# Two-layer attention and expert block on one core: score masks at the end of a group of banks, diagonals cleared on GpSimd, and a new order of expert pieces

## The chip, the cores and the metric

The program runs on one core of one Trainium2 chip. The metric is the device time of one launch in microseconds, lower is better.

## What is computed

The input is x with 8 batches of 512 tokens of 256 features. Two layers follow each other, and each adds an attention and a mixture of experts, both computed from the same normalized input:

```python
xn = _layernorm(x)
x = x + L0_attn(xn) + L0_ffn(xn)   # 16 heads of 16; softmax; 8 experts, each token takes 4
xn = _layernorm(x)
x = x + L1_attn(xn) + L1_ffn(xn)   # sparsemax attention; L1_ffn: grouped-query attention, then 8 experts, each token takes 2
# each attention: causal scores of 512 x 512 for every head
scores = q @ k.T * scale            # masked above the diagonal
attn = softmax(scores)              # L1_attn: maximum(scores - tau, 0), tau from the sorted row (sparsemax)
ctx = attn @ v
# each expert: out = down(act(gate(x)) * up(x))
```

So there are three attentions over 8 batches and 16 heads (the first layer's, called "mla" in the kernel, the grouped-query one, "gqa", and the sparsemax one, "spm") and two layers of experts.

## The kernel before

**Pairs.** The kernel walks through 192 pairs of heads G: 8 pairs for each batch n = G // 8, first the 8 batches of mla, then of gqa, then of spm. p = G % 8 is the pair's place in its batch. The order of all instructions is written out by hand: each engine has its own program (TensorE as `pe`, VectorE as `dve`, ScalarE as `act`, GpSimd as `pool`, the loads on `sp`), they go through the pairs in the same order, and semaphores join them.

**Scores.** A pair has its scores twice. The "q" scores (line 586) have queries in the partitions; VectorE takes their row maxima (`maxima`, lines 1800 and 1798, the latter a MAX8 for sparsemax). The "k" scores (line 589) have keys in the partitions; ScalarE turns them into the probabilities `pt` (`probabilities`, line 1447), and TensorE multiplies `pt` by V (`outputs`, line 658). Each kind is 6 units, 3 for each of the two heads j, of 512, 512 and 256 columns, and each unit fills one PSUM bank. In front of the scores of a unit stands a mask matmul (line 579), which puts the large negative values above the diagonal into the bank (`start=True`); the scores then add to it. VectorE's maxima of pair G + 1 and ScalarE's probabilities of pair G are made in the same round.

**Banks.** PSUM has 8 banks. A `Ring` hands out the banks of S (scores) and of X (transposes, projections, outputs) in turn; whoever takes a bank waits until its former user has read it (`S.former`). In a pair without experts ("alone") both rings have 4 banks; in a pair with experts X has 2 and S has 3 (banks 5 to 7), and banks 2 to 4 take the expert matmuls:

```python
wide, narrow = (banks[0:4], banks[4:8]), (banks[0:2], banks[5:8])
```

**Experts.** The tokens are sorted into tiles of 256, 71 tiles in the first layer and 39 in the second. A tile is six pieces: gate, up and down, each for m = 0 and 1; each piece is 12 matmuls of 256 columns (line 533 for gate and up, line 553 for down). `plan` lays them into pairs: 15 pieces in each of the pairs 21 to 49 (mla) and 6 in each of the pairs 138 to 176 (spm). The pieces of a pair are cut into the six parts q = 0 to 5 of `pair_with_experts`, between which the pair's scores, transposes and outputs stand. After the up piece VectorE makes the product t (line 1648), ScalarE its high part ah (line 1350), and GpSimd the low part al (`low`, line 1128); the down piece of the same tile and m reads both. `xl` (line 1603) is the low part of a tile's input.

**The rest of the round.** `turn_qk` transposes q and k of pair G + 1 (line 507) once GpSimd has stacked them (`stack`, lines 1161 to 1180). `outputs_by_rows` turns the outputs back (line 507, oT). `project` makes the next batch's projections. In the first pairs GpSimd also makes square roots by powers (`head_rms`, lines 1204 and 1210), which VectorE's `norm_heads` (line 1749) waits for, and scatters token rows for the experts (`route_scatter`, line 1264, 8 scatters in each of the pairs 3 to 18).

Of the kernel before, what the change touches and what calls it, by code (L numbers as in the profile page):

```python
# [23 lines left out]
P = 128  # L24
# [4 lines left out]
ALU = mybir.AluOpType  # L29
# [4 lines left out]
B, T, D = 8, 512, 256  # L34
# [24 lines left out]
FIRST_GATHERS = 55  # L59
KINDS = ["mla"] * B + ["gqa"] * B + ["spm"] * B  # L60
# [16 lines left out]
PT_AT = {0: 0, 3: 512, 1: 640, 2: 1024}  # L77
# [70 lines left out]
def build(nc, dram, outs, ctx):  # L148
# [232 lines left out]
    def pipeline(kinds, its, mems, em=None, general=False):  # L381
# [49 lines left out]
        dve_step, pool_step = new("dve_step"), new("pool_step")  # L431
# [46 lines left out]
        scatter_at = {2 * b + 3 + half: [(b, half)] for b in range(B) for half in range(2)} if em else {}  # L478
# [7 lines left out]
        with block as block:  # L486

            @block.tensor
            def _(pe):
# [68 lines left out]
                def experts(G, q):  # L558
                    for what, s, i in plan[G][q]:
# [7 lines left out]
                def scores(which, G, units):  # L567

                    mem = mems[kinds[G // NP]]
                    for u in units:  # L570
                        name = (which, G, u)
                        S.add(name, "dve" if which == "q" else "act")
                        if S.former[name]:
                            pe.wait_ge(*S.former[name])
                        bank = S.bank(name)
                        unit = (Q_UNITS if which == "q" else K_UNITS)[u]

                        diag = min(first + (P * blk if which == "q" else 0) for _, blk, first, _ in unit)
                        pe.matmul(bank[:, diag:diag + P * len(unit)], ident_bf[:, :],  # L579
                                  masks_bf[:, 0 if which == "q" else 1, 0:len(unit), :].rearrange("p n k -> p (n k)"),  # L580
                                  start=True, stop=False, skip_group_check=True)
                        for n, (j, blk, first, width) in enumerate(unit):
                            end = n == len(unit) - 1
                            ks = mem["ksT"][key_at[G] % 2][j]
                            if which == "q":
                                mm = pe.matmul(bank[:, first:first + width], mem["qsT"][:, P * blk:P * (blk + 1)],  # L586
                                               ks[:, 0:width], start=False, stop=end, skip_group_check=True)
                            else:
                                mm = pe.matmul(bank[:, first:first + width], ks[:, P * blk:P * (blk + 1)],  # L589
                                               mem["qaT"][:, T - width:T], start=False, stop=end, skip_group_check=True)  # L590
                        mm.then_inc(s_full, 1)
# [54 lines left out]
                def outputs(G):  # L646
# [3 lines left out]
                    pe.wait_ge(s_act, S.count[("k", G, NU - 1)])  # L650
# [114 lines left out]
                def pair_with_experts(G):  # L765
# [28 lines left out]
                    experts(G, 5)  # L794
                    if is_at(n - 1, "spm") and p == 1:
                        attention_out(n - 1)
                    if nxt and 1 <= p <= NT:
                        project(n + 1, p - 1)
# [70 lines left out]
            def _(sp):  # L869
# [56 lines left out]
                def experts(G, q):  # L926
                    for what, s, i in plan[G][q]:
# [193 lines left out]
            def _(pool):  # L1121
# [9 lines left out]
                def experts(G, q):  # L1131
# [1298 lines left out]
```

## Time and profile before

| | before |
|---|---|
| time, median of 3 runs | 3224.46 us (3221.11 to 3225.25) |
| the profiled execution | 3229.72 us, span 3227.9 us, mean granted TensorE clock 0.956 |
| busy: PE, PEld | 2843.6 us (88%), 2276.0 us (71%) |
| busy: DVE, ACT, POOL | 2161.9 us (67%), 1622.1 us (50%), 1399.3 us (43%) |
| mask matmuls, line 579 | 2304, 581.2 us busy (matmuls overlap in the records) |

PE is TensorE's matmul, PEld its weight load, DVE is VectorE, ACT is ScalarE and POOL is GpSimd. Matmuls are pipelined, and their modelled durations overlap: the distance from one start to the next says what one costs. The pairs begin and end as follows (read from the first score matmul of each): pairs 0 to 20 alone, 0 to 423.9 us; pairs 21 to 49 with experts, to 1385.8; pairs 50 to 137 alone, to 2313.8; pairs 138 to 176 with experts, to 3055.4; pairs 177 to 191 alone, to 3227.9.

### The profile page before, as it was taken

What the parts mean: (1) busy time and instruction counts of PE and PEld (TensorE: products, weight loads), DVE (VectorE), ACT (ScalarE), POOL (GpSimd) and SP (SyncE); (2) the same over time, 40 slices, a digit from 0 to 9 for tenths busy, and PEclk for the clock granted to TensorE, in tenths of its full rate; (3) what the DMA queues carried; (4) which work ended last, traced back from release to release, by engine and by line L of the source; (5) the groups of instructions that cost most, each with busy time, mean ns of one, the idle gap of its engine ahead of it and who ended that gap; (6) DMA issues with size and microseconds to landing.
All of it is one profiled execution on the core that took longest, in us unless ns stands there. A gap on an engine that the chain in (4) does not pass through costs nothing. (4 is left out here: it accounts for less than half of the span.)

```text
span 3227.9 us, 61041 instructions
## 1 busy us (share of the span) xinstructions
PE 2843.6 (88%) x21398; PEld 2276.0 (71%) x21398; DVE 2161.9 (67%) x6229; ACT 1622.1 (50%) x3388; POOL 1399.3 (43%) x1941
## 2 busy tenths in 40 slices
PE   3877789999999999979888888898799999999986
PEld 1555578888888888856666666666588888888864
DVE  3876778678777767756777777766645544454576
ACT  1544444444444454445555555565455545545553
POOL 3587742343233233275556666322222222222377
PEclk8878899999999999989999999999899999999999
DMA  2465567678777777613333334210365555565445
GB/s 80 143 232 185 203 242 304 260 267 316 278 271 278 273 289 271 255 30 61 94 92 106 106 105 106 90 67 22 138 226 197 221 200 203 197 228 193 137 99 125
DMA packets 192067, 580.11 MB, mean 180 GB/s; under 512 B 22857, under 2 KB 144657, under 8 KB 157457
## 3 DMA queue, kind: packets, MB, share of 16 engines
q1 hardware_dynamic: 154896, 525.03, 44.1%
q0 software_dynamic: 36864, 51.14, 7.7%
q8 instruction: 175, 2.87, 0.3%
q14 instruction: 132, 1.07, 0.1%
HBM read 450.14 MB, written 125.96 MB: 178 GB/s over the span
## 5 line engine op out<-in xcount | busy, mean ns | idle before, releaser
L1128 POOL TENSOR_TENSOR al<-t,ah 128x512 fp32r<-128x512 f32 x220 | 285.6, 1298 | 989.4 <-ACT ah L1350 989.4
L579 PE MATMUL bank<-masks_bf,ident_bf 128*128 128x128 bf16 (+1 forms) x2304 | 581.2, 252 | 113.9 <-DVE st L1800 52.8
L533 PE MATMUL bank<-xh,gu 128*128 128x256 f32 x3520 | 628.3, 285 | 10.0 <-issue 5.1
L1800 DVE TENSOR_REDUCE st<-bank 128x1 f32<-128x512 f32 (+3 forms) x1024 | 422.2, 480 | 202.3 <-PE bank L586 202.1
L1447 ACT ACTIVATE pt<-bank 128x512 f32<-128x512 f32 (+1 forms) x1152 | 511.4, 540 | 91.2 <-PE bank L589 89.7
L533 PEld LDWEIGHTS bank<-xh,gu 128*128 128x128 f32 x3520 | 505.2, 190 | 19.6 <-issue 13.5
L579 PEld LDWEIGHTS bank<-masks_bf,ident_bf 128*128 128x128 bf16 x2304 | 225.6, 98 | 391.6 <-DVE st L1800 112.6
L586 PE MATMUL bank<-ksT,qsT 128*128 128x512 f32 (+3 forms) x1536 | 438.1, 382 | 0.0
L589 PE MATMUL bank<-qaT,ksT 128*128 128x512 f32 (+3 forms) x1536 | 435.3, 392 | 0.0
L1455 ACT ACTIVATE oT<-bank 128x512 f32<-128x512 f32 x192 | 114.4, 596 | 547.9 <-PE bank L658 547.9
L533 PE MATMUL bank<-xl,gu 128*128 128x256 f32 x1760 | 352.5, 282 | 0.0
L507 PE MATMUL bank<-ident,qst 128*128 128x128 f32 x1536 | 239.5, 284 | 82.6 <-POOL kst L1180 52.7
L1350 ACT ACTIVATE ah<-t 128x512 fp32r<-128x512 f32 x220 | 138.8, 631 | 309.4 <-DVE t L1641 271.9
L586 PEld LDWEIGHTS bank<-ksT,qsT 128*128 128x128 f32 x1536 | 285.3, 206 | 4.0 <-issue 1.3
L589 PEld LDWEIGHTS bank<-qaT,ksT 128*128 128x128 f32 x1536 | 281.3, 204 | 0.0
L553 PE MATMUL bank<-dn,ah 128*128 128x256 f32 x1760 | 259.8, 291 | 22.3 <-issue 13.6
L533 PEld LDWEIGHTS bank<-xl,gu 128*128 128x128 f32 x1760 | 272.0, 190 | 0.0
L507 PEld LDWEIGHTS bank<-ident,qst 128*128 128x128 f32 x1536 | 183.9, 146 | 120.7 <-POOL kst L1180 62.4
L658 PE MATMUL bank<-pt,V 128*17 128x512 f32 (+3 forms) x3072 | 260.8, 460 | 0.7 <-ACT pt L1447 0.7
L1798 DVE MAX8 top<-bank 128x8 f32<-128x512 f32 (+3 forms) x512 | 213.2, 482 | 55.2 <-PE bank L586 52.4
L553 PEld LDWEIGHTS bank<-dn,ah 128*128 128x128 f32 x1760 | 227.3, 192 | 31.6 <-issue 31.6
L1224 POOL DMA_INDIRECT acc<-ys_scratch,slots x128 | 203.3, 1588 | 44.0 <-issue 43.6
(253 smaller groups left out, 5124.7 us busy)
## 6 DMA issues: line engine op xcount, KB each, us to landing
gu<-wu_scratch SPq DMA_DIRECT2D x110, 2056.0 KB, 7.9
dn<-wd_scratch SPq DMA_DIRECT2D x110, 1024.0 KB, 9.5
xs<-xs_scratch SPq DMA_DIRECT2D x110, 264.0 KB, 9.0
ys_scratch<-yb SPq DMA_DIRECT2D x110, 256.0 KB, 9.8
raw<-in_gu SPq DMA_DIRECT2D x16, 1024.0 KB, 5.6
wu_scratch<-hi SPq DMA_DIRECT2D x16, 1024.0 KB, 9.5
wu_scratch<-lo SPq DMA_DIRECT2D x16, 1024.0 KB, 12.8
xs_scratch<-empty SPq DMA_DIRECT2D x32, 264.0 KB, 5.3
```

The source lines that it names most:

```text
L507: mm = pe.transpose(bank[:, P * n:P * (n + 1)], b, ident[:, :])
L533: mm = pe.matmul(bank[:, TS * h:TS * (h + 1)], gu[:, col:col + P], x[s % 2][:, TS * k:TS * (k + 1)], start=(n == 0), stop=(n == len(terms) ...
L553: mm = pe.matmul(down_bank[:, D * half:D * (half + 1)], a[s % 2][:, j // 2, tok:tok + P], dn[:, part + D * j:part + D * (j + 1)], start=(n ...
L579: pe.matmul(bank[:, diag:diag + P * len(unit)], ident_bf[:, :], masks_bf[:, 0 if which == "q" else 1, 0:len(unit), :].rearrange("p n k -> ...
L586: mm = pe.matmul(bank[:, first:first + width], mem["qsT"][:, P * blk:P * (blk + 1)], ks[:, 0:width], start=False, stop=end, skip_group_che ...
L589: mm = pe.matmul(bank[:, first:first + width], ks[:, P * blk:P * (blk + 1)], mem["qaT"][:, T - width:T], start=False, stop=end, skip_group ...
L658: mm = pe.matmul(bank[q0:q0 + HD + 1, P * kb:T], V[n % 2][:, kb, vh, :], pt[:, j, PT_AT[kb]:PT_AT[kb] + T - P * kb], start=(kb < 2), stop= ...
L1128: pool.tensor_tensor(em["al"][s % 2][:, m, :], em["t"][g % 2][:, :], em["ah"][s % 2][:, m, :].bitcast(F32), ALU.subtract).then_inc(al_read ...
L1224: pool.indirect_dma_start(acc[:, NT * b + t, :], None, ys_dram, at, compute_op=ALU.add).then_inc(gathered[i], 16)
L1447: act.activation(to, frm, ACT.Relu if kind == "spm" else ACT.Exp).then_inc(s_act, 1)
L1798: ins = dve.max(top[:, 0, r, :], bank[:, first:first + width])
L1800: ins = dve.reduce_max(st[:, 0, r:r + 1], bank[:, first:first + width], AX.X)
```

## The change

Six parts of code change.

1. `scores` takes its units in groups, of 3 units where S has 3 banks and of 2 where it has 4. All waits for the group's banks stand before its first matmul. Then come the scores of all its units, and at the end one mask matmul for each unit, which now adds to the scores; only this last one tells the reader that the bank is full.
2. In pairs with experts (68 pairs) the k units are `bare`: they have no mask matmul. GpSimd's new `clear` sets the entries of `pt` above the diagonal to zero with four affine_selects of 256 columns per pair, and `outputs` waits for these (`pt_ready`). The blocks of `pt` lie in another order (`PT_AT`) so that two diagonal blocks can be reached with one stride. The clears stand on GpSimd behind the low parts of part q = 2.
3. In the first layer the pieces of a tile go gate 0, up 0, gate 1, down 0, up 1, down 1, where before they went gate, up, down, gate, up, down (the downs are those of the tile before).
4. In mla pairs with experts, `project` (and ScalarE's `take_projected`) stands before the last piece of part q = 5, not behind it.
5. The scatters of pairs 3 to 18 are 10, 5, 5, 10, 10, 8, 10, 5, 5, 5, 5, 10, 12, 12, 12 and 4, where before they were 8 in each; the sum is 128 as before.
6. `norm_heads(0, 4:H)` on VectorE stands behind the maxima and the shift of pair 1, where before it stood ahead of pair 0.

The core of the diff (the other engines' `experts` take the same slice):

```diff
@@ constants
+FIRST_SCATTERS = (10, 5, 5, 10, 10, 8, 10, 5, 5, 5, 5, 10, 12, 12, 12, 4)
-PT_AT = {0: 0, 3: 512, 1: 640, 2: 1024}
+PT_AT = {0: 0, 2: 512, 3: 768, 1: 896}
@@ plan
-                for m in range(2):
-                    work += [("gate", s, m), ("up", s, m)] if cur else []
-                    work += [("down", s - 1, m)] if prev else []
+                ups = [[("gate", s, m), ("up", s, m)] if cur else [] for m in range(2)]
+                downs = [[("down", s - 1, m)] if prev else [] for m in range(2)]
+                if layer == 0:
+                    work += ups[0] + ups[1][:1] + downs[0] + ups[1][1:] + downs[1]
+                else:
+                    work += ups[0] + downs[0] + ups[1] + downs[1]
@@ PE, scores
-                    for u in units:
-                        name = (which, G, u)
-                        S.add(name, "dve" if which == "q" else "act")
-                        if S.former[name]:
-                            pe.wait_ge(*S.former[name])
-                        bank = S.bank(name)
...
+                    bare = which == "k" and G in plan
+                    side, width_of = 0 if which == "q" else 1, Q_UNITS if which == "q" else K_UNITS
+                    size = 3 if len(S.banks) == 3 else 2
+                    for group in [units[i:i + size] for i in range(0, len(units), size)]:
+                        for u in group:
+                            S.add((which, G, u), "dve" if which == "q" else "act")
+                            if S.former[(which, G, u)]:
+                                pe.wait_ge(*S.former[(which, G, u)])
+                        for u in group:
+                            bank, unit = S.bank((which, G, u)), width_of[u]
+                            for n, (j, blk, first, width) in enumerate(unit):
...
+                            if bare:
+                                mm.then_inc(s_full, 1)
+                        for u in group if not bare else ():
+                            bank, unit = S.bank((which, G, u)), width_of[u]
+                            diag = min(first + (P * blk if which == "q" else 0) for _, blk, first, _ in unit)
+                            pe.matmul(bank[:, diag:diag + P * len(unit)], ident_bf[:, :],
+                                      masks_bf[:, side, 0:len(unit), :].rearrange("p n k -> p (n k)"),
+                                      start=False, stop=True, skip_group_check=True).then_inc(s_full, 1)
@@ PE, outputs
-                    pe.wait_ge(s_act, S.count[("k", G, NU - 1)])
+                    if G in plan:
+                        pe.wait_ge(pt_ready, 4 * (1 + sorted(plan).index(G)))
+                    else:
+                        pe.wait_ge(s_act, S.count[("k", G, NU - 1)])
@@ PE, pair_with_experts (ACT's has the same with take_projected)
-                    experts(G, 5)
...
+                    if is_at(n, "mla"):
+                        experts(G, 5, slice(0, -1))
+                        if nxt and 1 <= p <= NT:
+                            project(n + 1, p - 1)
+                        experts(G, 5, slice(-1, None))
+                    else:
+                        experts(G, 5)
...
@@ POOL
+                def clear(G, j):
+
+                    pt = mems[kinds[G // NP]]["pt"]
+                    pool.wait_ge(s_act, S.count[("k", G, NU // 2 * (j + 1) - 1)])
+                    for first, size in ((0, 1024), (768, 256)):
+                        blocks = pt[:, j, first:first + size].rearrange("p (n q) -> p n q", n=2)[:, :, 0:P]
+                        pool.affine_select(out=blocks, in_=blocks, pattern=[[0, 2], [1, P]], compare_op=ALU.is_ge, fill=0.0,
+                                           base=0, channel_multiplier=-1).then_inc(pt_ready, 1)
...
                     if G in plan:
-                        for q in range(2, 6):
+                        experts(G, 2)
+                        clear(G, 0)
+                        clear(G, 1)
+                        for q in range(3, 6):
                             experts(G, q)
...
-                    for b, half in scatter_at.get(G, ()):
-                        route_scatter(b, half)
+                    for b, t, k in scatter_at.get(G, ()):
+                        route_scatter(b, t, k)
@@ DVE
+                    if G == 0 and is_at(0, "mla"):
+                        norm_heads(0, slice(4, H))
...
-                if kinds[0] == "mla":
-                    norm_heads(0, slice(4, H))
                 for G in range(steps):
```

The first place is TensorE in a pair alone, at the q scores of the next pair (ksT and qsT are the keys and the queries, the numbers in names only tell buffers and semaphores apart, and s_dve and s_act count the banks that VectorE and ScalarE have read). Before:

```order
L579 MATMUL bank<-masks_bf,ident_bf 128x128 [waits s_act_301,k_half_309,cast_170]
L586 MATMUL bank<-ksT_53,qsT 128x512
L579 MATMUL bank<-masks_bf,ident_bf 128x256 [waits s_act_301]
L586 MATMUL bank<-ksT_53,qsT 128x384
L586 MATMUL bank<-ksT_53,qsT 128x128
L579 MATMUL bank<-masks_bf,ident_bf 128x128 [waits s_act_301]
L586 MATMUL bank<-ksT_53,qsT 128x256
L579 MATMUL bank<-masks_bf,ident_bf 128x128 [waits s_act_301]
L586 MATMUL bank<-ksT_54,qsT 128x512
L579 MATMUL bank<-masks_bf,ident_bf 128x256 [waits s_dve_302]
```

After the change:

```order
L590 MATMUL bank<-ksT_53,qsT 128x512 [waits s_act_301,k_half_310,cast_170]
L590 MATMUL bank<-ksT_53,qsT 128x384
L590 MATMUL bank<-ksT_53,qsT 128x128
L601 MATMUL bank<-masks_bf,ident_bf 128x128
L601 MATMUL bank<-masks_bf,ident_bf 128x256
L590 MATMUL bank<-ksT_53,qsT 128x256 [waits s_act_301]
L590 MATMUL bank<-ksT_54,qsT 128x512
L601 MATMUL bank<-masks_bf,ident_bf 128x128 x2
L590 MATMUL bank<-ksT_54,qsT 128x384 [waits s_dve_302]
L590 MATMUL bank<-ksT_54,qsT 128x128
L590 MATMUL bank<-ksT_54,qsT 128x256
```

The two masks of a group moved behind the last score matmul of the group, and where a group's second bank is waited for, the wait stands ahead of the first bank's matmuls too.

The second place is TensorE in a sparse pair with experts, at the q scores of the next pair on both sides of a down piece (line 553 before is line 559 after; dn is the down weight, ah and al the two parts of the activation). Before:

```order
L579 MATMUL bank<-masks_bf,ident_bf 128x128 [waits s_act_301,k_half_309,cast_170]
L586 MATMUL bank<-ksT_55,qsT 128x512
L579 MATMUL bank<-masks_bf,ident_bf 128x256 [waits s_act_301]
L586 MATMUL bank<-ksT_55,qsT 128x384
L586 MATMUL bank<-ksT_55,qsT 128x128
L579 MATMUL bank<-masks_bf,ident_bf 128x128 [waits s_act_301]
L586 MATMUL bank<-ksT_55,qsT 128x256
L553 MATMUL bank<-dn_108,ah_88 128x256 [waits y_used_370,al_ready_368]
L553 MATMUL bank<-dn_108,ah_88 128x256 x7
L553 MATMUL bank<-dn_108,al_90 128x256 x4
L579 MATMUL bank<-masks_bf,ident_bf 128x128 [waits s_dve_302]
```

After the change:

```order
L590 MATMUL bank<-ksT_55,qsT 128x512 [waits s_act_301,k_half_310,cast_170]
L590 MATMUL bank<-ksT_55,qsT 128x384
L590 MATMUL bank<-ksT_55,qsT 128x128
L590 MATMUL bank<-ksT_55,qsT 128x256
L601 MATMUL bank<-masks_bf,ident_bf 128x128
L601 MATMUL bank<-masks_bf,ident_bf 128x256
L601 MATMUL bank<-masks_bf,ident_bf 128x128
L559 MATMUL bank<-dn_108,ah_88 128x256 [waits y_used_371,al_ready_369]
L559 MATMUL bank<-dn_108,ah_88 128x256 x7
L559 MATMUL bank<-dn_108,al_90 128x256 x4
L590 MATMUL bank<-ksT_56,qsT 128x512 [waits s_dve_302]
```

The masks stand as a block behind the scores of the three units, and the second half begins with a score matmul, ahead of which the waits of all three banks stand, where before it began with the mask of its first bank.

The third place is GpSimd in a sparse pair with experts (kst is the stack of keys, pt the probabilities). Before:

```order
L1177 MEMSET qst_50 128x8x2
L1180 COPY kst<-kst 128x8x16 [waits pool_step_304]
L1128 TENSOR_TENSOR al_90<-t_95,ah_88 128x512 [waits ah_ready_367]
L1128 TENSOR_TENSOR al_91<-t_94,ah_89 128x512 [waits ah_ready_367]
L1161 CAST qst_49<-qk_69 128x8x16 [waits loaded_169]
```

After the change:

```order
L1201 COPY kst<-kst 128x8x16 [waits pool_step_304]
L1149 TENSOR_TENSOR al_90<-t_95,ah_88 128x512 [waits ah_ready_368]
L1209 AFFINE_SELECT pt<-pt 128x2x128 [waits s_act_301]
L1209 AFFINE_SELECT pt<-pt 128x256
L1209 AFFINE_SELECT pt<-pt 128x2x128 [waits s_act_301]
L1209 AFFINE_SELECT pt<-pt 128x256
L1149 TENSOR_TENSOR al_91<-t_94,ah_89 128x512 [waits ah_ready_368]
```

Four clears were added between the low part of one piece and that of the next; the first of each two waits for ScalarE's probabilities of one head.

## Rows read from the trace of the kernel before

**Rows 1.** Windows, the five stages: us, busy of PE, PEld, DVE, ACT, POOL, PEclk, DMA share, GB/s.

```profile
0.00:423.90 423.90, 291.32 (x1700) 202.72 (x1704) 285.61 (x841) 178.33 (x363) 281.60 (x324) 0.81 0.49 173
423.90:1385.80 961.90, 891.06 (x7245) 807.97 (x7238) 712.84 (x1641) 447.55 (x882) 320.85 (x366) 0.99 0.72 272
1385.80:2313.80 928.00, 813.16 (x5872) 568.26 (x5876) 680.95 (x2175) 527.20 (x1188) 482.96 (x741) 0.96 0.30 82
2313.80:3055.40 741.60, 714.57 (x5615) 604.80 (x5608) 367.92 (x1208) 384.30 (x781) 183.47 (x359) 0.99 0.55 203
3055.40:3227.90 172.50, 133.47 (x977) 92.20 (x975) 114.58 (x366) 84.72 (x179) 130.38 (x154) 0.96 0.53 108
```

**Rows 2.** Timeline of PE in a pair alone: start, us, engine, line, what.

```profile
1502.29 0.22 PE L579 MATMUL bank<-masks_bf,ident_bf 128*128 128x128 bf16 x1
...
1504.31 0.23 PE L579 MATMUL bank<-masks_bf,ident_bf 128*128 128x128 bf16 x1
...
1504.64 1.27 PE L658 MATMUL bank<-pt,V 128*17 128x512 f32 x16
1505.85 0.23 PE L579 MATMUL bank<-masks_bf,ident_bf 128*128 128x128 bf16 x1
...
1507.88 0.38 PE L507 MATMUL bank<-ident,oT 128*128 128x128 f32 x2
```

**Rows 3.** Timeline of DVE and ACT in the same pair.

```profile
1502.90 3.27 DVE L1800 TENSOR_REDUCE st<-bank 128x1 f32<-128x512 f32 x8 [1.85 <-PE bank L586]
...
1506.47 2.62 ACT L1447 ACTIVATE pt<-bank 128x512 f32<-128x512 f32 x6
```

**Rows 4.** Waits of PEld, pairs 50 to 137: total us, times, longest.

```profile
PEld bank L579 <- DVE st L1800: 74.6, 192, 3.7
...
PEld bank L579 <- ACT ksT L1434: 25.5, 31, 1.2
```

**Rows 5.** Timeline of PE in a sparse pair with experts.

```profile
2535.98 0.23 PE L579 MATMUL bank<-masks_bf,ident_bf 128*128 128x128 bf16 x1
...
2537.00 0.40 PE L533 MATMUL bank<-xh,gu 128*128 128x256 f32 x2
2537.24 0.40 PE L533 MATMUL bank<-xl,gu 128*128 128x256 f32 x2
...
2538.43 0.23 PE L579 MATMUL bank<-masks_bf,ident_bf 128*128 128x128 bf16 x1
...
2539.39 1.11 PE L553 MATMUL bank<-dn,ah 128*128 128x256 f32 x8
...
2540.82 0.23 PE L579 MATMUL bank<-masks_bf,ident_bf 128*128 128x128 bf16 x1
...
2543.27 1.27 PE L658 MATMUL bank<-pt,V 128*17 128x512 f32 x16
...
2548.10 0.63 PE L507 MATMUL bank<-ident,oT 128*128 128x128 f32 x4 [1.06 <-DVE xl L1603]
```

**Rows 6.** Timeline of DVE and POOL in the same pair.

```profile
2539.58 3.48 DVE L1798 MAX8 top<-bank 128x8 f32<-128x512 f32 x8
...
2540.11 1.28 POOL L1128 TENSOR_TENSOR al<-t,ah 128x512 fp32r<-128x512 f32 x1 [3.21 <-ACT ah L1350]
```

**Rows 7.** Groups of GpSimd's instructions: busy us, mean ns, idle before.

```profile
L1180 POOL COPY kst<-kst 128x128 f32<-128x128 f32 x160 | 48.6, 304 | 10.1
```

**Rows 8.** Waits of PE, pairs 21 to 49.

```profile
PE bank L507 <- DVE xl L1603: 15.8, 8, 2.1
PE bank L553 <- issue: 13.6, 15, 1.2
...
PE bank L553 <- POOL al L1128: 4.7, 6, 0.8
...
PE bank L533 <- DMA gu<-wu_scratch: 2.1, 3, 1.2
```

**Rows 9.** Waits of all engines, pairs 0 to 20.

```profile
DVE qk_mla L1749 <- POOL qkn L1210: 15.6, 2, 13.0
```

More of the change, by code:

```diff
@@ L477, in pipeline @@
         per_batch = 16 * NT * CHOICES[0]
-        scatter_at = {2 * b + 3 + half: [(b, half)] for b in range(B) for half in range(2)} if em else {}
+        scatters = [(b, t, k) for b in range(B) for t in range(NT) for k in range(CHOICES[0])]
+        scatter_at = {3 + i: scatters[sum(FIRST_SCATTERS[:i]):sum(FIRST_SCATTERS[:i + 1])]
+                      for i in range(len(FIRST_SCATTERS))} if em else {}
         def routes(G, lag):
@@ L556, in down, with experts @@
                     mm.then_inc(y_full, 1)
-                def experts(G, q):
-                    for what, s, i in plan[G][q]:
+                def experts(G, q, some=slice(None)):
+                    for what, s, i in plan[G][q][some]:
                         if what == "gate":
@@ new lines, in scores @@
+                    bare = which == "k" and G in plan
[9 more added lines that the diff above has]
+                            for n, (j, blk, first, width) in enumerate(unit):
+                                end = bare and n == len(unit) - 1
+                                ks = mem["ksT"][key_at[G] % 2][j]
+                                if which == "q":
+                                    mm = pe.matmul(bank[:, first:first + width], mem["qsT"][:, P * blk:P * (blk + 1)],
+                                                   ks[:, 0:width], start=(n == 0), stop=end, skip_group_check=True)
+                                else:
+                                    mm = pe.matmul(bank[:, first:first + width], ks[:, P * blk:P * (blk + 1)],
+                                                   mem["qaT"][:, T - width:T], start=(n == 0), stop=end,
+                                                   skip_group_check=True)
+                            if bare:
[6 more added lines that the diff above has]
+                                      start=False, stop=True, skip_group_check=True).then_inc(s_full, 1)
@@ L924, in store_y, with experts @@
                     sp.dma_start(ys_blocks[s - FIRST_TILE[layer_of(s)]], em["yb"][s % 2][:, :, :]).then_inc(y_out[s % 2], 16)
-                def experts(G, q):
-                    for what, s, i in plan[G][q]:
+                def experts(G, q, some=slice(None)):
+                    for what, s, i in plan[G][q][some]:
                         if what == "up" and s + 2 < tiles_to(s):
@@ L1129, in low, with experts @@
                                        em["ah"][s % 2][:, m, :].bitcast(F32), ALU.subtract).then_inc(al_ready, 1)
-                def experts(G, q):
-                    for what, s, i in plan[G][q]:
+                def experts(G, q, some=slice(None)):
+                    for what, s, i in plan[G][q][some]:
                         if what == "up":
@@ L1364, in take_y, with experts @@
                                    scale=em["wsel"][s % 3][:, half:half + 1]).then_inc(y_used, 1)
-                def experts(G, q):
-                    for what, s, i in plan[G][q]:
+                def experts(G, q, some=slice(None)):
+                    for what, s, i in plan[G][q][some]:
                         if what == "up":
@@ L1506, in pair_with_experts @@
                     take_o(G)
-                    experts(G, 5)
-                    if n + 1 < nb and 1 <= p <= NT:
-                        take_projected(n + 1, p - 1)
+                    if is_at(n, "mla"):
+                        experts(G, 5, slice(0, -1))
+                        if n + 1 < nb and 1 <= p <= NT:
+                            take_projected(n + 1, p - 1)
+                        experts(G, 5, slice(-1, None))
+                    else:
+                        experts(G, 5)
+                        if n + 1 < nb and 1 <= p <= NT:
+                            take_projected(n + 1, p - 1)
                     if G + 1 in ends_at:
@@ L1649, in multiply, with experts @@
                                           ALU.mult).then_inc(a_ready, 1)
-                def experts(G, q):
-                    for what, s, i in plan[G][q]:
+                def experts(G, q, some=slice(None)):
+                    for what, s, i in plan[G][q][some]:
                         if what == "gate":
```

42 lines of the change are left out of this document (13 added, 29 removed).

## The prediction

> **What bounds the kernel now.** I read the windows first, cut at the pairs where the kernel changes its manner [rows 1]. TensorE is busy in 93 to 96% of the two stretches with experts (891 of 962 us, 715 of 742), in 88% of pairs 50 to 137 alone, and in 69% of the first. So where experts run the time is what TensorE has to issue, and a matmul taken out is time won unless a wait takes its place. Alone, TensorE and VectorE (681 of 928 us) hand PSUM banks to each other, and it is the handing over that counts.
>
> The timeline of one pair alone shows that [rows 2, 3]. The q scores begin at 1502.29 and end where the outputs begin, 1504.64: 2.35 us for 6 units. VectorE's first maximum begins at 1502.90, 0.61 later, and its 8 reductions then run on end for 3.27 us, 0.41 each. The last unit (1504.31) waits for a bank whose maxima end at 1502.90 plus the first three reductions and some signalling, 1.41 after VectorE's start. The k scores last from 1505.85 to 1507.88, 2.03 us; ScalarE starts 0.62 after them and reads 2560 columns in 2.62 us. The chain of the round goes q scores, outputs, k scores, transposes, all on TensorE. The waits of the weight loads say that this pair is typical: 192 waits at line 579 for VectorE's maxima, over two per pair [rows 4]. Of the 88 pairs, 31 wait for ksT as well, 25.5 us in all: there a delay of TensorE's scores can be partly absorbed.
>
> In a sparse pair with experts, call T the start of the first q half, 2538.43 [rows 5, 6]. A half of q scores costs 0.96 (to the down piece at 2539.39), a k half 1.02 (2535.98 to 2537.00), and a matmul of 256 columns 0.12 (two from 2537.00 to 2537.24). VectorE's maxima begin at T+1.15 and run on end for 3.48 us through both halves; the second q half begins on TensorE at T+2.39, the outputs at T+4.84. GpSimd's low part ends at T+2.96.
>
> **The change, pair by pair.**
>
> *Groups in pairs alone (part 1).* The same matmuls are issued, but a bank is full only when the whole group of two has been scored. At 0.12 us per 256 columns the first group's 1024 columns take 0.24 + 0.18 + 0.12 = 0.54 before the first mask, where before the first bank's last matmul was issued at 0.03 and took a slot to 0.35. The first bank is therefore full some 0.25 later, and VectorE starts at about 0.86 rather than 0.61. It needs the same 1.41 until the second bank is free, and the third group, which now waits for both banks ahead of its first matmul, starts at 2.27. Its 384 + 128 + 256 columns and two masks take about 0.66, so the q scores end at 2.93: **+0.58**. Likewise for k: ScalarE starts at 0.87 and has read the first two units (1024 of 2560 columns) 1.05 later; with the signal the third group starts at 2.0 and ends at 2.66: **+0.63**. I take 1.15 a pair, 101 us over 88 pairs. What absorbs it is the pairs that wait for ksT or for GpSimd: about half of the 25.5 us and a little more, 15. **Pairs 50 to 137: +86.** The last 15 pairs, partly bound by GpSimd's gathers (130 of 172 us busy [rows 1]), get 0.85 each: **+13**. The bounds are 0 (if everything else in the round were late enough) and the full 1.2, which is 124 over 103 pairs.
>
> By the Trainium skill (TensorE: Matmul & The Clock Gate, back-to-back issue gap) a stream of weight loads and matmuls of 128 columns goes at 81 ns each, where the rows here show 0.11 to 0.12; by it the third groups would be some 0.1 shorter each, and the sum about 18 us less. The row decides.
>
> *Masks out of the k halves with experts (part 2).* Bare, a k half is 1280 columns, 0.60 to 0.66, against 1.02: 0.38 won, 0.76 a pair. In pairs 21 to 49, 29 pairs, **−22**. VectorE's q maxima there have two or three pieces of 1.4 us between the halves, so a group of three waits for nothing.
>
> *Order of pieces and projection (parts 3, 4).* Down pieces in pairs 21 to 49 wait 13.6 (put down to issue, but ahead of a matmul that waits for al) and 4.7 us for GpSimd [rows 8]. With another piece between up and down this goes, −18. But a_ready, by which the next gate weights are loaded, comes one piece later for one of two pieces; three waits for gu already exist, 2.1 us, so the slack is thin. I give half back, +9: **−9**. The waits for xl (15.8) stay: the projection's move only changes which instruction meets them. Stage sum **−31**; bounds −15 (all of the waits come back) and −42.
>
> *Sparse pairs with experts (parts 1, 2).* The masks again give 0.76. Against it, the second q half now waits for all three banks at once, that is for the maxima of the whole first half: T+1.15+1.74 = T+2.89, where TensorE arrives at T+2.36. So it stalls 0.53, and VectorE then idles until the second half's first mask, but ends its maxima at about T+5.5, ahead of what needs them. Net some −0.16 a pair. The down piece's product t and the transposes (the wait of 1.06 at 2548.10) follow TensorE and shift with it. 39 pairs: **−6**.
>
> *The clears.* No row shows an affine_select. Each is 256 columns; the nearest rows are a copy of 128 columns, 0.304 [rows 7], and a two-input operation of 512, 1.28 [rows 6]: bounds 0.30 and 1.3; a line through both gives 0.63 for 256, which I take. Four of them behind the low part end at T+2.96+2.52 = T+5.48; TensorE reaches the outputs at T+4.84+0.53 = T+5.38. So 0.1 of wait, with the signal 0.16: **+6** over 39. They fall free below 0.6; from there each 0.1 us costs 0.4 a pair, 16 us. In pairs 21 to 49 two and a half times the pieces lie in between, and GpSimd is busy 321 of 962 us: hidden. The next low part stands behind the clears, but its down piece is a pair later.
>
> By the Trainium skill (GPSIMD Engine Reference, 3.1 Elementwise) an element costs about 2.6 cycles with two inputs, 1.8 in the best loop; at 1.2 GHz that is 0.38 to 0.55 us for 256 columns, and the clears would be hidden. For the 512-column row with two inputs it gives 1.11 us, and the row has 1.28; no row here shows a one-input select, so the line stands.
>
> *First pairs (parts 5, 6).* VectorE stands 13.0 us in norm_heads behind GpSimd's powers with the maxima of pair 1 ready behind it [rows 9]. Moved, it does some 5 us of that work in the gap: **−5**. The scatters have the same sum, and GpSimd is busy 282 of 424 us there [rows 1]; I count neither their spreading nor the group's lateness, since those pairs wait for GpSimd. Bounds −12 and +8.
>
> Sum: +86 + 13 − 31 − 6 + 6 − 5 = **+63** on the profiled execution of 3229.7 us, 5.3 above the median of the runs: 3224.5 + 63 = 3287; I say **3286**.
>
> **The rivals.**
>
> *A, the forecast: TensorE waits in the third groups.* For it: the banks' turn is fixed, and 192 waits stand there already. Own range: 0.9 to 1.2 a pair alone and the bounds of the other terms, 3255 to 3320. Chance 0.66.
>
> *B, the clears are dear.* At 1.0 us each they end at T+6.96, and the outputs wait 1.58 a pair, 62 us over 39 in place of 6: 3342. For it: the two-input row, 1.28 for 512 columns, if most of it were a fixed cost [rows 6]; against it: the copy's 0.304, which bounds what is fixed [rows 7]. It decides from 0.9 up. Chance 0.12.
>
> *C, the groups cost half.* If the round alone is held by something else, the 0.45 left are 46 us over 103 pairs, against −36 from the rest: 3234. Against it: 88% of TensorE busy. Chance 0.12.
>
> *D, faster.* The place is the same third group: if the delay of VectorE's start is only 0.1 (a mask at the end is short, and VectorE could be let in sooner after it than after a score matmul of 512) and the third group's start is met by banks free earlier, a pair alone loses 0.2, 21 us, against −36, with cheap clears −6 more: 3203 to 3210. It decides from 0.35 us a pair alone down (36 / 103). Against it: the wait for the second bank exists today, and nothing makes it shorter. Chance 0.10.
>
> **How the numbers follow.** The likeliest is A, 3286. The range must leave out no more than 2 in 10: it drops D and the outer half of B and takes in C: 3232 to 3338. This kernel's measurement tells 0.2%, 6.4 us, from no change. Slower is A, B and most of C, 0.86; C's lower end gives 0.05 within 0.2%; D is 0.09 and over.
>
> **What the profile of the changed kernel would show.** Alone: q scores of 2.9 us and k scores of 2.65, with waits of the third group for st and for pt; stretches of about 1014 us for pairs 50 to 137 and 186 for the last. Pairs 21 to 49 in 931 us, with new waits for gu and few at the down piece. Pairs 138 to 176 in 742, with VectorE idle about 0.9 us between its two groups of MAX8, and a short wait of the outputs for GpSimd; the affine_select at 0.63 us. First stretch 419. The prediction is wrong if the pairs alone are not longer by 0.9 or more, or if an affine_select takes over 0.9 us.

## The result and the profile after

The changed kernel takes 3316.62 us (median of 4 runs, 3313.60 to 3321.54), the kernel before 3222.78 us, measured beside it: the ratio is 1.0288, with an interval of 1.0271 to 1.0305. It is slower by 94 us; the forecast was 3286 us, in a range of 3232 to 3338.

The page of the changed kernel begins so (share of the span, count of instructions):

```profile
span 3314.7 us, 61380 instructions
...
PE 2793.5 (84%) x20990; PEld 2293.6 (69%) x20990; DVE 2177.6 (66%) x6229; ACT 1647.5 (50%) x3388; POOL 1499.9 (45%) x2213
```

TensorE has 408 matmuls less, and the span is 86.8 us longer: the work went down and the waiting up. The windows, cut at the same pairs as [rows 1] (the cuts ahead of pairs 21 and 138 lie 0.1 to 0.3 us behind the start of the outputs of the pair before, and not at a first score matmul; they do so in every run below, so the stretches compare):

```profile
0.00:425.20 425.20, 288.87 (x1700) 204.01 (x1704) 288.12 (x841) 182.34 (x363) 281.13 (x324) 0.84 0.51 178
425.20:1353.30 928.10, 864.99 (x7070) 807.31 (x7062) 717.21 (x1641) 447.47 (x881) 366.50 (x482) 0.99 0.75 279
1353.30:2377.10 1023.80, 806.60 (x5872) 581.68 (x5876) 690.22 (x2175) 545.48 (x1187) 484.41 (x741) 0.96 0.28 75
2377.10:3125.00 747.90, 695.32 (x5378) 603.07 (x5379) 366.57 (x1208) 383.56 (x781) 239.13 (x514) 1.00 0.54 200
3125.00:3314.70 189.70, 137.70 (x981) 97.51 (x979) 115.53 (x366) 88.62 (x179) 128.72 (x154) 0.94 0.48 98
```

| pairs | before | forecast | after | difference, forecast and measured |
|---|---|---|---|---|
| 0 to 20, alone | 423.9 | 419 | 425.2 | −5, +1.3 |
| 21 to 49, experts | 961.9 | 931 | 928.1 | −31, −33.8 |
| 50 to 137, alone | 928.0 | 1014 | 1023.8 | +86, +95.8 |
| 138 to 176, experts | 741.6 | 742 | 747.9 | 0, +6.3 |
| 177 to 191, alone | 172.5 | 186 | 189.7 | +13, +17.2 |

Every stretch of pairs alone is longer. In pairs 50 to 137 the instructions are as many as before and the granted clock is the same (0.96 both times); in the first pairs it was 0.84 against 0.81, in the last 0.94 against 0.96. The pair alone of [rows 2, 3], in the timeline of the changed kernel:

```profile
1479.42 0.85 PE L590 MATMUL bank<-ksT,qsT 128*128 128x512 f32 x3
1480.11 0.34 PE L601 MATMUL bank<-masks_bf,ident_bf 128*128 128x128 bf16 x2
...
1480.44 3.38 DVE L1837 TENSOR_REDUCE st<-bank 128x1 f32<-128x512 f32 x8 [2.05 <-PE bank L601]
...
1481.94 0.64 PE L590 MATMUL bank<-ksT,qsT 128*128 128x384 f32 x3 [1.01 <-DVE st L1837]
1482.42 0.34 PE L601 MATMUL bank<-masks_bf,ident_bf 128*128 128x256 bf16 x2
1482.69 1.27 PE L673 MATMUL bank<-pt,V 128*17 128x512 f32 x16
1483.89 0.79 PE L593 MATMUL bank<-qaT,ksT 128*128 128x512 f32 x3
...
1484.85 1.85 ACT L1478 ACTIVATE pt<-bank 128x512 f32<-128x512 f32 x4 [0.22 <-PE bank L601]
...
1486.08 0.64 PE L593 MATMUL bank<-qaT,ksT 128*128 128x128 f32 x3 [0.74 <-ACT pt L1478]
1486.56 0.34 PE L601 MATMUL bank<-masks_bf,ident_bf 128*128 128x256 bf16 x2
1486.73 0.61 PE L513 MATMUL bank<-ident,oT 128*128 128x128 f32 x4
```

The q scores take 3.27 us (1479.42 to 1482.69) where they took 2.35, the k scores 2.84 where they took 2.03. In each, the third group stands and waits: 1.01 us for VectorE, 0.74 for ScalarE. VectorE starts 1.02 us after the first score matmul, where it started 0.61 after the first mask. The waits of TensorE over pairs 50 to 137 (us in all, times, longest) say that it is so throughout:

```profile
PE bank L590 <- DVE st L1837: 91.0, 77, 3.7
PE bank L593 <- ACT pt L1478: 61.5, 88, 1.0
PE bank L590 <- DVE top L1835: 19.7, 11, 5.3
```

The first and the third line are the waits for VectorE's maxima (st, and top in sparse pairs), 77 and 11, one in each of the 88 pairs; in the kernel before TensorE's matmuls waited 26.7 us in 13 waits for st and 6.7 in 3 for top. The second line, again one wait in each pair, has no counterpart among the matmuls of the kernel before. Its weight loads did wait for ScalarE's pt, 83 times and 13.0 us in all; they now do 88 times, 74.6 us.

The pair shown is one of the first layer's attention. In the 64 grouped-query pairs alone (64 to 127), which are most of the 88, the medians counted from the traces are 0.89 us from the first score matmul to VectorE's start (0.61 before), 3.14 for the q scores (2.36) and 2.84 for the k scores (2.03).

A sparse pair with experts, to be read beside [rows 5, 6]:

```profile
2604.10 0.86 PE L590 MATMUL bank<-ksT,qsT 128*128 128x512 f32 x4
...
2605.52 1.68 DVE L1835 MAX8 top<-bank 128x8 f32<-128x512 f32 x4
...
2606.06 1.27 POOL L1149 TENSOR_TENSOR al<-t,ah 128x512 fp32r<-128x512 f32 x1 [3.12 <-ACT ah L1381]
...
2607.28 1.49 POOL L1209 TENSOR_SCALAR_AFFINE_SELECT pt<-pt 128x256 f32<-128x256 f32 x4
...
2607.35 0.87 PE L590 MATMUL bank<-ksT,qsT 128*128 128x512 f32 x4 [0.67 <-DVE top L1835]
...
2608.33 1.69 DVE L1835 MAX8 top<-bank 128x8 f32<-128x512 f32 x4 [1.13 <-PE bank L601]
2609.81 1.27 PE L673 MATMUL bank<-pt,V 128*17 128x512 f32 x16
```

VectorE's maxima, one run of 3.48 us before, are two runs with 1.13 us of idle time between them, and the second q half waits 0.67 for the first. The four clears take 1.49 us together and are done at 2608.77, 1.04 before the outputs at 2609.81. Over the whole of pairs 138 to 176 no wait of the outputs for GpSimd is in the trace, so the clears hold TensorE up nowhere there.

### The profile page after: what moved, and what is told of

It reads as the page before. It is cut to its first block and busy times, and to the rows that moved or that the text cites. A ratio compares the mean times of both kernels' runs of the same rounds, so it can differ in the third digit from the quotient of the medians.

```text
span 3314.7 us, 61380 instructions
## 1 busy us (share of the span) xinstructions
PE 2793.5 (84%) x20990; PEld 2293.6 (69%) x20990; DVE 2177.6 (66%) x6229; ACT 1647.5 (50%) x3388; POOL 1499.9 (45%) x2213
## 5 line engine op out<-in xcount | busy, mean ns | idle before, releaser
L539 PE MATMUL bank<-xh,gu 128*128 128x256 f32 x3520 | 654.9, 290 | 19.4 <-DMA gu<-wu_scratch 5.7
L1478 ACT ACTIVATE pt<-bank 128x512 f32<-128x512 f32 (+1 forms) x1152 | 522.4, 529 | 90.6 <-PE bank L601 65.0
L1837 DVE TENSOR_REDUCE st<-bank 128x1 f32<-128x512 f32 (+3 forms) x1024 | 430.1, 481 | 205.9 <-PE bank L601 203.4
L590 PE MATMUL bank<-ksT,qsT 128*128 128x512 f32 (+3 forms) x1536 | 366.2, 353 | 223.9 <-DVE st L1837 124.4
L590 PEld LDWEIGHTS bank<-ksT,qsT 128*128 128x128 f32 x1536 | 259.0, 197 | 286.4 <-DVE st L1837 139.0
L593 PE MATMUL bank<-qaT,ksT 128*128 128x512 f32 (+3 forms) x1536 | 362.0, 350 | 91.4 <-ACT pt L1478 90.6
L593 PEld LDWEIGHTS bank<-qaT,ksT 128*128 128x128 f32 x1536 | 237.4, 194 | 153.4 <-ACT pt L1478 108.9
L601 PE MATMUL bank<-masks_bf,ident_bf 128*128 128x128 bf16 x1896 | 301.6, 248 | 0.0
L673 PE MATMUL bank<-pt,V 128*17 128x512 f32 (+3 forms) x3072 | 270.2, 474 | 0.5 <-ACT pt L1478 0.5
L1182 POOL CAST qst<-qk 128x128 fp32r<-128x128 f32 x128 | 45.0, 351 | 390.4 <-PE bank L513 381.1
```

Of the source, the lines that this page charges most:

```text
L539: mm = pe.matmul(bank[:, TS * h:TS * (h + 1)], gu[:, col:col + P], x[s % 2][:, TS * k:TS * (k + 1)], start=(n == 0), stop=(n == len(terms) ...
L673: mm = pe.matmul(bank[q0:q0 + HD + 1, P * kb:T], V[n % 2][:, kb, vh, :], pt[:, j, PT_AT[kb]:PT_AT[kb] + T - P * kb], start=(kb < 2), stop= ...
L1478: act.activation(to, frm, ACT.Relu if kind == "spm" else ACT.Exp).then_inc(s_act, 1)
L1837: ins = dve.reduce_max(st[:, 0, r:r + 1], bank[:, first:first + width], AX.X)
```

## The experiments

Each run changes one thing in the kernel that it starts from; the comparisons by stretch are between single profiled executions. e1 to e4 ran on one chip, e5 to e8 on a second, e9 and e10 on a third; the kernel before took 3242.28, 3226.22 and 3226.27 us on them, and no execution of it was profiled on the first. Stretches with the same code came out up to 6 us apart in pairs 50 to 137 (922.4 in e7, 922.5 in e5, 924.2 in e6, 926.0 in e8, 927.9 in e10 and 928.0 in the kernel before, which all have the same scores there), 7 us apart in pairs 21 to 49 (928.1 in the changed kernel, 935.4 in e2), 4 us apart in pairs 0 to 20 and 1 us apart in pairs 138 to 176. Only more than that is read as a difference.

**One unit in a group, everywhere (e1) and in pairs alone only (e2).**

```diff
-                    size = 3 if len(S.banks) == 3 else 2
+                    size = 1                                   # e1
+                    size = 3 if len(S.banks) == 3 else 1       # e2
```

> The changed kernel with groups of one unit everywhere: each unit waits for its own bank, then come its scores and its mask. All else stays. My theory (banks are told full too late and waited for too early) gives pairs 50 to 137 about 930 us (1023.8 in the changed kernel), the last 15 pairs 173 to 177 (189.8), pairs 138 to 176 about 730 (747.8), since the stall of the second q half goes too, pairs 21 to 49 unchanged at 928: a span of about 3190. The rival, that the loss in pairs alone lies in what is left of the change there (the mask adding to the scores rather than the scores to the mask, the other layout of pt), leaves pairs 50 to 137 above 1000 and the span above 3290.

> Groups of one unit in pairs alone only; pairs with experts keep groups of three. My theory: pairs 50 to 137 at 930 us, the last pairs at 175, pairs 138 to 176 still 748, a span of about 3207. The difference of pairs 138 to 176 to the run with one unit everywhere is what the group of three costs there: I expect 15 to 20 us. If the rival is right that the clears or the layout of pt take back what the masks gave in pairs 138 to 176, both runs have the same 748 there.

e1 took 3190.7 us, a ratio of 0.9844 (0.9827 to 0.9860) to the kernel before. Its pairs 50 to 137 take 939.1 us, its last pairs 171.0 and pairs 138 to 176 718.6. e2 took 3230.11 us, with 935.9, 174.8 and 748.1. So the groups are the loss in pairs alone: 85 of the 96 us. With experts the groups of three cost 748.1 − 718.6 = 29.5 us, where I had expected 15 to 20. The whole of e2 is longer than I expected too, a span of 3228.3 us against 3207, because its pairs 0 to 20 (434.1) and 21 to 49 (935.4) are. The rival that the clears or the layout of pt hold the sparse pairs falls with e1's 718.6. What is open is that the pairs 50 to 137 of e1 and e2 are still 11 and 8 us above the kernel before.

**The two halves of a group: early waits only (e3), late masks only (e4).** In e3 each unit's mask follows its scores; in e4 each unit's wait stands ahead of its own scores.

```diff
 # e3: the mask moves into the loop over scores
-                        for u in group if not bare else ():
...
+                            if not bare:
...
+                                pe.matmul(bank[:, diag:diag + P * len(unit)], ident_bf[:, :],
 # e4: one loop for waits and scores
                             if S.former[(which, G, u)]:
                                 pe.wait_ge(*S.former[(which, G, u)])
-                        for u in group:
                             bank, unit = S.bank((which, G, u)), width_of[u]
```

> Groups as in the changed kernel, but only their waits stand together: each unit's mask follows its scores at once, so a bank is told full as soon as before. In pairs alone VectorE should start some 0.3 us sooner than in the changed kernel, and the third group still waits for two banks. By my step-by-step sum a pair alone then loses 0.9 rather than 1.6 us against the kernel before: pairs 50 to 137 at about 985 us. If the early waits cost nothing by themselves, they come to 930; if they are the whole loss, to 1020.

> Groups as in the changed kernel, but each unit waits for its own bank ahead of its own scores; the masks stay at the group's end. In pairs alone the first unit of the third group can be scored while the second bank is still read, but its mask comes behind the second unit's wait. By my sum a pair alone loses about 0.9 us too: pairs 50 to 137 at about 985 us. In pairs 138 to 176 the first units of the second q half no longer wait for the last bank: 735 to 742. If late masks cost nothing by themselves, pairs 50 to 137 come to 930; if they are the whole loss, to 1020.

Windows of e3, pairs 50 to 137 and pairs 138 to 176:

```profile
1369.60:2357.70 988.10, 825.29 (x5872) 587.43 (x5876) 685.12 (x2175) 542.33 (x1188) 483.38 (x741) 0.96 0.29 78
2357.70:3105.60 747.90, 694.80 (x5381) 596.10 (x5374) 369.58 (x1208) 381.69 (x781) 239.40 (x515) 1.00 0.54 200
```

Windows of e4, the same pairs:

```profile
1367.80:2342.00 974.20, 841.97 (x5872) 586.95 (x5876) 682.85 (x2175) 535.43 (x1188) 485.11 (x741) 0.96 0.29 78
2342.00:3067.10 725.10, 694.81 (x5377) 599.62 (x5377) 367.26 (x1208) 383.52 (x780) 239.64 (x514) 1.00 0.57 208
```

Over e1's 939.1, the early waits cost 49 us in pairs alone and the late masks 35, together 84: what both cost in the changed kernel (1023.8 − 939.1 = 84.7). That the sum is so exact is luck: in the medians of pairs 64 to 127 the two blocks of scores are 0.88 us longer with the early waits, 0.72 with the late masks and 1.39 with both, so 0.2 a pair of them overlap. With experts they do not add up at all: the early waits alone bring back the whole 29 us (747.9), the late masks 6.5 (725.1, where I had expected 735 to 742).

**The mask ahead of its scores again, unit by unit (e5).** This is the `scores` of the kernel before, with bare k units where experts run:

```diff
-                    for group in [units[i:i + size] for i in range(0, len(units), size)]:
+                    for u in units:
...
+                        if not bare:
...
+                                      start=True, stop=False, skip_group_check=True)
                         for n, (j, blk, first, width) in enumerate(unit):
+                            begin, end = bare and n == 0, n == len(unit) - 1
```

> The changed kernel with the scores of the kernel before, unit by unit and the mask ahead of its scores, except that the k units of pairs with experts stay bare. With groups of one and the mask behind, pairs 50 to 137 took 939 us where the kernel before took 928, and its shortest pairs 7.37 where before 7.19. If that rest is the mask's place (VectorE and ScalarE let in some 0.1 us later at each block of scores), this kernel gives 928 to 930 there, 718 in pairs 138 to 176, 925 in pairs 21 to 49, and a time of 0.981 of the kernel before. If the rest is the layout of pt or the chip, pairs 50 to 137 stay at 939 and the ratio at 0.984.

3161.71 us, a ratio of 0.9794 (0.9778 to 0.9810): faster than both kernels. Its windows of pairs 50 to 137 and 138 to 176:

```profile
1346.30:2268.80 922.50, 806.26 (x5872) 564.57 (x5876) 680.80 (x2175) 527.02 (x1188) 482.90 (x741) 0.96 0.31 83
2268.80:2983.80 715.00, 686.42 (x5382) 591.65 (x5374) 364.79 (x1208) 381.46 (x780) 239.60 (x515) 1.00 0.57 210
```

The rest was the mask's place. The difference of these two executions, 939.1 − 922.5 = 16.6 us, is the upper end: between e1 and e2 (939.1 and 935.9) and the six executions with the mask ahead (922.4 to 928.0) lie 8 to 17 us over 88 pairs. Counted pair by pair it is plainer. In pairs 64 to 127 the medians of e1 and e2 agree, and so do those of e5 to e8, e10 and the kernel before: with the mask behind, VectorE starts 0.69 us after the first matmul of the q scores and not 0.61, ScalarE 0.67 after that of the k scores and not 0.63, and the two blocks last 2.49 and 2.10 us and not 2.36 and 2.03. That is 0.20 us a pair, and the shortest pairs are 7.19 us again where e1's had 7.37. The layout of pt, which e5 keeps, has no part in it, for e10 keeps it too and takes 927.9.

**The kernel of e5 with the old order of pieces (e6), with the projection in its old place (e7), with the first pairs as before (e8).**

```diff
 # e6
-                if layer == 0:
-                    work += ups[0] + ups[1][:1] + downs[0] + ups[1][1:] + downs[1]
-                else:
-                    work += ups[0] + downs[0] + ups[1] + downs[1]
+                work += ups[0] + downs[0] + ups[1] + downs[1]
 # e7, on PE and ACT
-                        experts(G, 5, slice(0, -1))
+                        experts(G, 5)
                         if nxt and 1 <= p <= NT:
                             project(n + 1, p - 1)
-                        experts(G, 5, slice(-1, None))
 # e8
+FIRST_SCATTERS = (8,) * 16
...
+                if kinds[0] == "mla":
+                    norm_heads(0, slice(4, H))
                 for G in range(steps):
```

> The kernel of the run with masks first and single units, with the first layer's pieces in the old order. Pairs 21 to 49: the masks alone should leave 940 us (962 less 22), so 937 to 940, and the waits of the down piece for al (18 us in the kernel before) should be there again, those for gu gone. If the order brings nothing, pairs 21 to 49 stay at 925.

> The kernel of the run with masks first and single units, with the projection of mla pairs behind the last piece again. By my sum this part does nothing: pairs 21 to 49 within 2 us of that run. The rival: it is what took the waits for xl away (15.8 us in the kernel before), then they are 8 to 16 us longer.

> The kernel of the run with masks first and single units, with 8 scatters in each pair and norm_heads ahead of pair 0 again. I forecast 5 us for these two; so pairs 0 to 20 are 5 us longer than in that run, and the time 0.15% more. If they bring nothing, both are the same within 3 us.

Pairs 21 to 49 take 927.9 us in e5, 950.7 in e6 and 926.5 in e7. The order of pieces brings 23 us where I had expected e6 to lose 9 to 12 (937 to 940). TensorE's waits in these pairs, e6:

```profile
PE bank L510 <- DVE xl L1632: 28.7, 14, 2.1
PE bank L556 <- issue: 18.4, 16, 1.9
...
PE bank L536 <- DMA gu<-wu_scratch: 4.8, 7, 1.1
PE bank L556 <- POOL al L1141: 4.0, 5, 0.8
...
PE bank L556 <- ACT yb L1386: 3.8, 14, 0.4
```

and e5:

```profile
PE bank L513 <- DVE xl L1635: 28.4, 14, 2.1
...
PE bank L539 <- DMA gu<-wu_scratch: 6.5, 8, 1.8
PE bank L539 <- DVE gc L1647: 5.1, 5, 1.7
```

All 26.2 us of waits at the down piece (line 556) are gone in e5, and some 6 came back at gate and up (line 539): gu 1.7 more, gc 4.6 more. The projection's place is worth nothing, as forecast: e7 waits for xl at two lines, 16.1 and 9.6 us, where e5 waits 28.4 at one. e8 takes 422.3 us for pairs 0 to 20, and the kernel before 423.9, where e5, e6, e7 and e10, alike there, take 418.4, 418.6, 414.6 and 414.4: so 4 to 9 us more. e8's ratio of 0.9809 (0.9791 to 0.9826) overlaps that of e5, so the timed runs don't settle it.

**Clears made twice (e9, on the changed kernel), masks kept (e10, on e5).**

```diff
 # e9
-                    for first, size in ((0, 1024), (768, 256)):
+                    for r, first, size in ((0, 0, 1024), (0, 768, 256), (1, 0, 1024), (1, 768, 256)):
+                        if r:
+                            pool.wait_ge(pt_ready, 8 * sorted(plan).index(G) + 4 * j + 2)
...
-                        pe.wait_ge(pt_ready, 4 * (1 + sorted(plan).index(G)))
+                        pe.wait_ge(pt_ready, 8 * (1 + sorted(plan).index(G)))
 # e10
-                    bare = which == "k" and G in plan
+                    bare = False
...
-                        clear(G, 0)
-                        clear(G, 1)
```

> The changed kernel with every clear made twice: 8 affine_selects a pair. In the changed kernel four start 0.36 us apart, and in pair 148 they end 1.15 us before the outputs. Doubled they take 1.45 us more and two signals, so the outputs of a sparse pair with experts should wait 0.4 to 0.5 us: pairs 138 to 176 at 764 us (747.8 in the changed kernel). That would be the rival of the dear clears, reached at the size that my sum gives. If they stay hidden it is 748; if GpSimd's later start on the other low part holds the down piece, over 775.

> The kernel of the run with masks first and single units, but with the masks of the k units with experts kept and no clears: what is left of the change is the order of pieces, the projection's place and the first pairs. The old order of pieces cost 23 us in that run, the masks' removal with the old order brought 11 (962 to 951). If the order takes away the waits at the down piece (22 us in the kernel before, with those for al and yb) and adds those for gu and gc, pairs 21 to 49 take 943 to 947 us, and the masks bring 16 to 20 with the new order, more than the 11 with the old. Pairs 138 to 176: 741, as before.

e9 takes 774.6 us for pairs 138 to 176, 26.7 more than the changed kernel, with these waits:

```profile
PE bank L673 <- POOL pt L1211: 21.6, 38, 0.8
PE bank L513 <- DVE xl L1642: 19.2, 18, 1.1
```

I had expected 764. The first wait, of the outputs for the clears, is not in the changed kernel at all; it is 0.57 each, not far from the 0.4 to 0.5. The other 5 us stand behind it: the transposes of e9 wait 19.2 us for xl, where those of the changed kernel wait 12.2 for qaT and 1.0 for xl. e10 takes 944.3 us for pairs 21 to 49 and 741.6 for pairs 138 to 176, inside what I expected. So the order alone brings 961.9 − 944.3 = 17.6 us, and the masks with the new order 944.3 − 927.9 = 16.4, and in pairs 138 to 176 741.6 − 715.0 = 26.6.

## Why the prediction was right, and where its terms were off

**Groups in pairs alone: right, and too small.** The place, the kind of wait and the sign are as forecast, and the experiments show the cause: undone alone, the groups give 85 of the 96 us back, and the mask's place, 8 to 17 us, covers the rest. The mis-sized terms are the parts of the sum for one pair. In the pair shown the q scores were to take 2.93 us and take 3.27: VectorE starts 1.02 after them, not 0.86, the third group 1.50 after that rather than 1.41, and it lasts 0.75 rather than 0.66. The k scores were to take 2.66 and take 2.84. That is +1.73 in the two blocks where I had 1.2, and in this pair (10.14 us against 8.63 in the kernel before, from one start of the line that copies qaT to the next) 1.51 of it remain. In the more numerous grouped-query pairs VectorE's start, 0.89, is nearly the 0.86 of the sum; there the error lies in what follows, and the two blocks are 1.60 longer. I had let VectorE in after the mask as soon as after a score; e1 and e2 against e5 give 0.20 a pair for the mask's place alone. Over 88 pairs 1.51 would be 133 us, of which 96 arrived; by this estimate from one pair the other waits absorbed some 37, where I had 15 of 101. That the two errors cancel for the most part is luck.

By the Trainium skill (TensorE: Matmul & The Clock Gate, back-to-back issue gap), with its 81 ns for a matmul of 128 columns in a stream with weight loads, the sum would by the prediction's estimate have come out 18 us lower, at 45; the spans differ by 87. In the trace of the kernel before, transposes of 128 columns in f32 stand 0.11 us apart and expert matmuls of 256 columns 0.12. The rows of the trace were the better guide.

**Masks and order in pairs 21 to 49: the sum right, its split wrong.** −34 against −31. The step that failed is that each mask taken out is time won there (−22). With the old order it is 961.9 − 950.7 = 11: the matmuls come sooner, and the waits that stand behind them grow by 7, those at the down piece from 22.2 (13.6 + 4.7 and 3.9 for yb) to 26.2 and those for xl from 25.4 (the 15.8 of [rows 8] and 9.6 at the projections) to 28.7. The second failure is the order's term, −9: I gave half of its 18 us back to new waits for gu. With the masks kept it brings 17.6 in full, without them 23, and gu and gc take back some 6. (The 5 us between the two are less than the 7 by which executions differ here; that they belong to the waits at the down piece is argued from the lists, not shown by the times.) That the stage's sum came out is luck: the two errors cancelled.

**Pairs 138 to 176: two errors that nearly cancel.** The masks bring 26.6 (I had 0.76 times 39, 30). The second q half waits 27.0 us for maxima in the changed kernel, 0.69 each in 39 waits, where I had 0.53 each, 21. With the late masks the transposes wait for ScalarE's qaT, which I had not seen:

```profile
PE bank L590 <- DVE top L1835: 27.0, 39, 1.1
PE bank L513 <- ACT qaT L1482: 12.2, 17, 0.8
PE bank L513 <- DVE xl L1640: 1.0, 1, 1.0
```

This wait stands in e4 as well (12.4 us, 17 times) and not in e5. It is no cost on top, for it stands where the transposes had waited for xl, which in e5 is 19.2 us in 18 waits. What the groups add to the waits is the first line. With the masks' place they cost 747.9 − 715.0 = 33 us where I had 24 (30 less the net of 6). The clears, for which I gave +6, bring no wait.

**The clears.** The step "a line through both gives 0.63 for 256" failed: four take 1.49 us, 0.37 each. The rival of dear clears had the right mechanism and no cause to happen. At twice the number it does: 26.7 us. By the Trainium skill (GPSIMD Engine Reference, 3.1 Elementwise) the best loop, 1.8 cycles for an element, gives an estimate of 0.38 for 256 columns. The trace agrees with that figure, 0.37, and my sum would have been 6 lower in this term with it.

**The first and the last pairs.** The moves of parts 5 and 6 bring 4 to 9 us, if the single profiled executions are believed (I had 5). The changed kernel doesn't show it (425.2), because its groups cost time there too, which I had left out: on one chip e9, with the groups, takes 423.9 and e10, without them, 414.4. e1 and e2 do not bear on this: on their chip pairs 0 to 20 take 430.0 and 434.1 without any groups, and why is open. The last pairs lose 17.2 rather than 13, for the reason of the pairs alone.

**The rivals.** C (half the loss) had 46 us over the 103 pairs; they lost 113 (95.8 and 17.2). D (faster) needed a loss of at most 0.35 a pair alone; it was 1.1 on average. Without the groups the rest of the change is worth more than the 36 us that C and D set against the loss: e5 is 65 us faster than the kernel before.

## What to carry to other kernels

Where two engines hand buffers to each other, waiting for a group of them at once and telling them full at once can cost on both sides: in the pairs alone here both halves cost, with experts nearly all of it was the early wait. A buffer should be waited for as late and released as early as its own work allows, even when the instructions stay the same in number. A change of several parts should be split by the stretch in which each works: here one part, the groups with the masks behind, cost 158 us of span (3314.7 less the 3157.1 of e5) and the others won 71 (3227.9 less that), and only that part had to be undone. Taking work out ahead of a wait is worth less than its price until the wait goes too, so the two should be tried together.

## What the runs showed that I had not expected

A mask matmul of 128 or 256 columns behind its scores instead of ahead of them costs 0.2 us a pair, though the instructions are the same. An affine_select of 256 columns on GpSimd takes 0.37 us, hardly more than a copy of 128 (0.304 [rows 7]), so that 408 mask matmuls could be replaced by it with no wait for it in pairs with experts. Making the clears twice also lengthened pairs 21 to 49 from 928.1 to 938.9 us, little more than the 7 us by which two executions of the same code differ there. Of these 11 us 4.9 are waits of the outputs for GpSimd, 8 of them, which the changed kernel doesn't have; the rest is left open.
